# Linear attention stage: TensorE runs the new pair's shared-layer products ahead of the old pair's transposition

## The reference, cut to what matters

```
q, k0, k1, v0, v1 = x @ (Wq, Wk0, Wk1, Wv0, Wv1) + biases
q, k0, k1         = silu(.) + 0.5, divided by the norm of each group of 8 numbers
state             = (k0^T v0, masked to 8x8 blocks) * (k1^T v1)     # per sequence
att               = (layer norm of (q @ state)) @ Wo + bo
shared            = (silu(x @ shared_gate) * (x @ shared_up)) @ shared_down
```

## Time and profile before

| | us |
|---|---|
| median of 3 runs | 1534.5 |
| lowest and highest run | 1530.03, 1534.76 |
| the profiled execution's own time | 1530.27 |
| its span, first to last instruction | 1528.4 |
| mean granted TensorE clock, share of full | 0.909 |

### The profile page before, as it was taken

One profiled execution on the slowest core, in us unless ns is written; L12 is line 12 of the kernel. 1 busy time (PEld: TensorE's weight loads), 2 busy tenths in 40 slices (PEclk: granted clock), 3 DMA queues, 4 the chain that ended last, 5 costly groups with the idle time before them and its releaser, 6 DMA issues. The chain is left out here.

```text
span 1528.4 us, 29193 instructions
## 1 busy us (share of the span) xinstructions
PE 1209.7 (79%) x7783; PEld 912.8 (60%) x7784; DVE 1069.0 (70%) x3641; ACT 787.0 (51%) x2010; POOL 653.9 (43%) x1270
## 2 busy tenths in 40 slices
PE   3999999999600899999999744568888888698883
PEld 2777777778500677777777533346666666355552
DVE  3777777777697677777777367757777777266663
ACT  1666576665300565665665455646666656233331
POOL 3344343443100354554555456714444433155555
PEclk9999999999855999999999855579999999699997
DMA  3432433424100122122122155534444443355552
GB/s 130 143 133 87 143 103 120 139 88 147 40 0 24 42 58 57 39 60 55 39 61 48 18 167 183 164 131 142 144 148 148 154 155 125 99 165 151 161 167 76
DMA packets 159336, 162.58 MB, mean 106 GB/s; under 512 B 21030, under 2 KB 138509, under 8 KB 159296
## 3 DMA queue, kind: packets, MB, share of 16 engines
q1 hardware_dynamic: 144016, 132.98, 27.6%
q0 software_dynamic: 14848, 26.77, 6.3%
q10 hardware_dynamic: 432, 2.38, 0.4%
HBM read 76.33 MB, written 71.04 MB: 96 GB/s over the span
## 5 line engine op out<-in xcount | busy, mean ns | idle before, releaser
L376 ACT ACTIVATE big<-ps,BHS 128x256 f32<-128x256 f32 x256 | 107.0, 470 | 59.6 <-PE ps L253 58.9
L388 ACT ACTIVATE pr<-ps,nmx 128x256 f32<-128x256 f32 x256 | 117.7, 475 | 32.2 <-DVE nmx L435 31.4
L253 PE MATMUL ps<-big,W 128*128 128x256 f32 x512 | 128.3, 395 | 5.7 <-ACT big L381 5.7
L266 PE MATMUL ps<-W,big 128*128 128x128 f32 x1024 | 130.7, 281 | 0.0
L266 PEld LDWEIGHTS ps<-W,big 128*128 128x128 f32 x1024 | 119.4, 192 | 13.8 <-ACT big L376 9.9
L2102 POOL DMA_INDIRECT out<-X,io x96 | 99.8, 1040 | 34.4 <-issue 34.4
L253 PEld LDWEIGHTS ps<-big,W 128*128 128x128 f32 x512 | 94.4, 194 | 26.2 <-ACT big L381 15.6
L435 DVE TENSOR_REDUCE nmx<-ps 128x2 f32<-128x512 f32 x128 | 82.3, 685 | 36.3 <-PE ps L288 36.3
L979 POOL DMA_INDIRECT ffn<-big,si x64 | 93.9, 1467 | 26.6 <-issue 26.6
L1944 PE MATMUL ps<-big,zT 128*128 x192 | 102.7, 617 | 2.4 <-DVE pr L2040 1.0
L2018 ACT ACTIVATE pr<-ps 128x256 f32<-128x256 f32 x96 | 36.8, 383 | 102.9 <-PE ps L1944 101.8
(11 more groups left out here) (244 smaller groups left out, 3370.1 us busy)
## 6 DMA issues: line engine op xcount, KB each, us to landing
srt<-big SPq DMA_DIRECT2D x16, 1584.0 KB, 5.8
X<-srt SPq DMA_DIRECT2D x24, 800.0 KB, 4.7
big<-we SPq DMA_DIRECT2D x16, 768.0 KB, 4.8
rowd<-big SPq DMA_DIRECT2D x32, 272.0 KB, 2.3
big<-x SPq DMA_DIRECT2D x64, 128.0 KB, 2.2
X<-big SPq DMA_DIRECT2D x64, 128.0 KB, 2.1
big<-we SPq DMA_DIRECT2D x16, 384.0 KB, 3.4
X<-srt SPq DMA_DIRECT2D x24, 256.0 KB, 4.8
```

What stands on the lines that cost most here:

```text
L253: last = pe.matmul(pb[2 * g + f // 2][:, f % 2 * S:(f % 2 + 1) * S], W0[:, l, 512 + f * P:512 + (f + 1) * P], zT2[:, g, :], start=True, st ...
L266: last = pe.matmul(pb[4 + g][:, t * C:(t + 1) * C], hT[:, g, f, t * P:(t + 1) * P], W0[:, l, 1024 + f * C:1024 + (f + 1) * C], start=(f == ...
L376: act.activation(hT[:, g, f, :], pb[2 * g + half][:, f % 2 * S:(f % 2 + 1) * S], ACT.Silu, bias=BHS[:, l, f:f + 1], scale=GELU).then_inc(s ...
L388: last = act.activation(pr[:, g, h, t, :], pb[2 * g + h][:, t * S:(t + 1) * S], ACT.Exp, bias=nmx[:, g, h * TPU + t:h * TPU + t + 1], accu ...
```

## The change

TensorE's list in steps 1 to 15 calls `hidden(i, 0)` before `turn(i, 0, 7)` and no longer behind it. Nothing else moves: the other engines' lists, the waits inside the two calls and the memory that they use stay as they are. Step 0 has no `turn` and step 16 no `hidden(i, 0)`, so they are as before.

```
                         if late:
                             attention(i, 1)
-                            turn(i, 0, 7)
                         if early:
                             hidden(i, 0)
                         if late:
+                            turn(i, 0, 7)
                             if early:
                                 pe.wait_ge(s["vb"], 2 * i + 2)
                             else:
```

## The result

The changed kernel takes 1541.1 us (median of 11 runs) and the kernel before 1534.6 (median of 11). The measured ratio is 1.0056, 95% interval 1.0037 to 1.0074: 0.56% slower, some 8.6 us, where 4.0 us were forecast. The plain medians lie only 6.5 us apart, so the size in us is less sure than the sign. A later set of runs gave 1.0065 (1.0052 to 1.0079). One run of the eleven, of 2497 us, was disturbed and is left out of the ratio. The profiled execution of the changed kernel took 1541.4 us with a span of 1539.6.

A forecast was written before the change was run, and what follows sets the result against it. The prediction took a chain of waits through several engines, without slack, to set the 18.21 us step. 14 steps by 0.24 plus 0.60 us gave 4.0 us, so 1534.5 becomes 1538.5 us, 0.26% slower; range 1533 to 1543.

The forecast's parts named there:

- The ring: Chain TensorE, VectorE, GpSimd, ScalarE and back, `states` to `states`, 18.21 us; without slack, so any delay lengthens the step.
- `turn` later by 0.30, `affine` by 0.24: Unit 0: `hidden` holds the array until 1140.11, so `turn` starts 0.30 us later and ScalarE's `affine` 0.24 us later.
- Step 1, 0.60 us: In step 1 `turn` is due sooner after `attention`, so `hidden` delays it by 0.60 us.
- The sum, 4.0 us: Whole kernel: 14 steps by 0.24 us plus 0.60 in step 1, 3.96, say 4.0 us; chance 0.70.
- a fall of the granted clock: A stretch at 1.2 GHz, `hidden` then taking 3.5 us, would cost more; set aside, no chance given.
- a new stop of TensorE of about 0.6 us: Sign in the profile: TensorE idle about 0.6 us ahead of L1639, ended by ScalarE's `affine`.
- what comes earlier: `out` of old unit 0 some 0.7 us earlier, `gu` about 1.7 us; also `result` and the scatter; worth nothing.
- Idle time filled: TensorE's 1.26 us idle ahead of `turn` of unit 0, 1.43 us with overlap, takes `hidden`'s 1.73 us; doesn't fit by 0.30.
- TensorE's wait for ScalarE's `norm`: Sign: no such wait left before `turn` of unit 0; TensorE's total falls from 21.7 to some 3 us.
- Faster by TensorE's order: Rival: TensorE's order after `turn` sets the step; `out` and all behind 0.7 us earlier, 10.5 us less, 1524; chance 0.05.
- Absorbed: Rival: an unseen slack in a link ends the 0.24 us; time stays 1534.5, or up to 2 us is left; chance 0.15.
- Drain and queueing: Rival: `hidden` waits for `attention` to drain and `turn` for `hidden`; 0.63 us a step, 9.8 us, 1544; chance 0.10.

The follow-up runs named there:

- the fillers: The kernel before, old order, with four throwaway products (1.73 us) between `attention` and `turn` of unit 0 in 15 steps: ratio 1.0029, 4.4 us more.
- the changed kernel with its clock kept: The changed kernel with two throwaway products (0.86 us) behind `shared`, ahead of `turn` of unit 1: ratio 1.0024.
- the first filler: The changed kernel with two throwaway products (about 0.86 us) between `turn` and `out` of old unit 0, 15 steps: ratio 1.0055.
- the changed order with the moved product: The changed kernel with the first product of `project` of new unit 0 put ahead of `states` of old unit 0: ratio 0.9997.

## Why the prediction was wrong

- **The ring** (links 1 to 6): right. Lengthening one link by 0.24 us lengthened each step by 0.24, and shortening another by 0.8 shortened it by 0.8.
- **`turn` later by 0.30, `affine` by 0.24:** right, 0.24 in the rows of after and, with the fillers, 3.4 us in 14 steps.
- **Step 1, 0.60 us:** 0.6 in the profile.
- **The sum, 4.0 us:** right for what it counts. The kernel that has the delay alone takes 4.4 us more (1.0029), and the changed kernel with its clock kept 3.7 us more (1.0024).
- **The step that failed** is in the rivals, where a fall of the granted clock is put at nothing: "both stretches show 1.00, and the change makes TensorE's longest stop shorter". The longest stop did get shorter; it went. But that was read from where `hidden` arrives and not from where it leaves. `hidden` stood between `turn` of unit 0 and `out`, and with 1.73 us of work it kept TensorE busy until `turn` of unit 1 was nearly due. Taken away, it left 0.75 us ahead of `out` and, since `shared` ended earlier too, 0.77 us ahead of `turn` of unit 1. The text saw the first ("a new stop of TensorE of about 0.6 us"), and put what comes earlier at nothing. It missed the second, and that this one stands next to the 0.93 us that were there before. Nor was the length of the longest stop a measure: the kernel before kept its clock through a stop of 1.26 us. In the profile the falls cost 5.9 of the 9.3 us between steps 1 and 15 (9.3 - 3.4) and most of what is left in the last step.
- **Idle time filled:** the prediction says that `hidden` fills a stop of 1.26 us. In the sum over the stage that is not so: TensorE's products are the same, the step got longer, so TensorE's idle time grew. It was only moved, from one stop with busy work on both sides into two small ones beside a third.
- **TensorE's wait for ScalarE's `norm`** was to fall from 21.7 us to some 3, and fell to 14.4: the same omission.
- **The rivals.** Faster by TensorE's order: no. Absorbed: no, at a quarter of a us no link had slack. Drain and queueing: the rows of after show `turn` behind `hidden` without a stop; the size forecast for it, 9.8 us, is near what was measured, which is luck: the cause was another.

The Trainium skill describes this in another kernel (TensorE: Matmul & The Clock Gate, A second HAM failure mode: psum-queue depth-cycling): short idles between groups of products can be frequent enough for the clock to swing to and fro. The trace agrees: between `turn` of unit 0 and the fall no stop of the changed kernel was longer than 0.93 us, and the clock swung in every second step. I had not weighed it.

What stays open: why the falls come in every second step and not in each, though every step has the same stops. Shifting the loop did not change it and a shorter step made it every third (the changed order with the moved product); with the first filler two falls came in neighbouring steps. How large the two stops must be is known only by the cases tried: 0.77 and 0.93 us bring falls, 0.45 and 0.93 don't. By what the chip decides the clock was not measured here. Of the 3.2 us by which the profiled execution was late before any changed instruction, about 1.5 go with a later return of the full clock; neither that nor the rest was looked into.

## What to carry to other kernels

When work is moved into an idle place, look at the place that it leaves: it may have been what kept TensorE running up to the next wait, and two small stops side by side can cost the clock for the products behind them. In a ring of waits, moved work must fit the place in whole (here 1.73 us into 1.43), or be split (one of four products ahead costs nothing, but gains nothing either). What pays is to shorten the ring itself, the chain of waits that comes back to its own start: one product of the next pair put ahead of the wait for `states` took 0.8 us off each step, 0.79% of the kernel.

## What the runs showed of the hardware that was not expected

- The granted clock fell to 1.2 GHz with TensorE stopped for no longer than 0.93 us at a time, and was back at 2.4 GHz after about 3.4 us of work. In that time `hidden` of unit 1 took 3.61 us, against 1.89 to 1.93 at 2.4 GHz.
- Throwaway products, off every path, made the kernel faster: the changed kernel at 1.0056 stands at 1.0024 with them ahead of `turn` of unit 1 and 1.0016 ahead of `out` of unit 1, but at 1.0055 with as many ahead of `out` of unit 0.
- An idle time shown ahead of a product understated the free place: 0.56 us shown were worth 0.8 us when filled (with VectorE's stop of 0.76 to 0.86 us filled too), and at 1.26 us shown, work of 1.73 us delayed `turn` by only 0.30, so 1.43 us were free.
